# A two-layer graph network on one core: GpSimd's layer-norm step set ahead of its row sums, VectorE's aggregation set ahead by one bank

## The chip, the cores and the metric

One NeuronCore of a Trainium2 chip runs the whole kernel. The metric is the device time of one execution in microseconds (us).

## The reference, cut to what matters

The inputs are x (128 graphs, 128 nodes, 64 features), adj (128 graphs, 128x128) and small weights. Layer 0 is an edge network, layer 1 a plain aggregation; each has a layer norm ahead of it and a residual.

```
h    = relu(layernorm(x))
mask = adj > 0
# layer 0, for every graph b, node j, neighbour k, hidden channel c (192)
P = h @ (W1a + W1b) + b1 ;  Q = h @ W1b
hm[b,j] = sum over k with mask[b,j,k] of relu(P[b,j] - Q[b,k])
x1  = x + hm @ W2 + deg * b2          # deg = number of neighbours
# layer 1
h2  = relu(layernorm(x1))             # the second layer norm
out = x1 + (adj @ h2) @ W3^T
```

About 12% of the entries of adj are set, so the kernel does not compute all 128x128 edges. It ranks the neighbours of each node and gathers them by rank.

## The kernel before, in words

**Ranks and slots.** A prologue of some 55 us turns adj into codes: the rank of each neighbour within its node. Every node has 16 regular slots, worked off in four chunks (i = 0 to 3) of four slots. A chunk fills one of three PSUM ring places of two banks, two slots to a bank. Nodes with more than 16 neighbours get overflow rows of three slots (the fifth chunk, i = 4).

**One step is one graph.** Each engine runs its own `step(b, u)`, written out for b = -3 to 131, in order, and the engines meet at semaphores only. The chunks of a graph pass through three engines:

- ScalarE writes P into the four slots of a ring place (`seed`, L530), the first chunk's at i = 0 and so on. The seed of chunk 1 (L540) waits until VectorE has consumed the whole chunk 3 of the graph before.
- TensorE adds -Q of the selected neighbours, by a product with one-hot matrices in two f16 parts (`gather`, L378), eight matmuls for a chunk.
- VectorE consumes a bank (`consume`, L763): relu and sum into acc. It does bank 0, then makes a piece of the one-hot matrices of the next four graphs (`prepare`, L749), then does bank 1. At fixed places between them stand its small tasks: L790 (bn_aggr of the second layer norm's statistics), L795 and L798 (which rows belong to which overflow row, for the next graph), L804, L680, the residual additions L813 and L816, and the statistics L819.

**TensorE's order** in a step b: chunk 0, four small matmuls (L420 to L423), chunk 1, the projections of graph b+1 and output products (L435 to L445), chunks 2 and 3, then at i = 3 a block of transposes (L454 to L470), then the overflow rows (L406, then L378 with onehot_row). The block of transposes sums the acc of graph b-1 (L464) with its overflow rows (L465), and forms adj @ h2 of graph b-3 (L470). Its waits stand ahead of what needs them: all the matmuls L464 and L465 stand behind `hm_row_ready`, and L470 behind `h2_ready`.

```
pe.wait_ge(summed, b * REGULAR)
pe.wait_ge(hm_row_ready, b)
...
pe.wait_ge(h2_ready, b - 2)
```

**GpSimd's order** in a step b: the three slots of graph b-1's overflow rows are added (L864, two additions, behind ScalarE's relu L562); then the second layer norm of graph b-3 (L873 variance plus eps, L874 minus the mean, L880 the power -0.5, L883 the shift), behind `mv_ready` from L790; then the start of the next graph's acc (L851), the low part of P (L890), bias and residual (L897, L900), and the split of a later graph's h (L906, L908).

**ScalarE's order** in a step: seeds 0, copies L550 and L556, seed 1, L562, L567, L570, seeds 2 and 3, L575, L576, then L583 (h2 = relu(x1 * rstd + shift), behind `norm2_ready` from L883) and L591, and then the next graph's seed 0.

Of the kernel before, what the change touches and what calls it, by code (L numbers as in the profile page):

```python
# [30 lines left out]
ALU = mybir.AluOpType  # L31
# [7 lines left out]
ROW_SLOTS = 3  # L39
# [14 lines left out]
def gnn_kernel(nc, x, adjT, W1a, W1b, b1, W2, b2, W3T, CONSTS, out):  # L54
# [15 lines left out]
    with ExitStack() as ctx:  # L70
# [550 lines left out]
        def _(dve):  # L621
# [138 lines left out]
            def consume(u, to, bank_, first):  # L760

                sums = acc[:, u % 2]
                return nc.vector.scalar_tensor_tensor(sums, slots[to][:, bank_], 0.0, start[:, :, :] if first else sums, ALU.max,  # L763
                                                      ALU.subtract if first else ALU.add)

            def step(b, u, looped=False, t=None):
                main = exists(b)
                at = bass.ds(b + 1, 1)
                for i in range(CHUNKS):
                    if i == 3 and main and exists(b + 1):  # L770
                        dve.wait_ge(p_ready, b + 2)
                        second_part(b + 1, u + 1)
                    if main and i < REGULAR:
                        if i == 0:
                            dve.wait_ge(start_ready, b + 1)
                            if exists(b - 2):
                                dve.wait_ge(transposed, b + 2)
                        else:
                            dve.wait_ge(summed, b * REGULAR + i)
                        dve.wait_ge(gathered, b * GATHERS + i * BANKS + 1)  # L780
                        consume(u, place(u, i), 0, i == 0).then_inc(half_summed, 1)
                    if i < REGULAR:
                        prepare(b, u, i)
                    if main and i < REGULAR:
                        dve.wait_ge(half_summed, b * REGULAR + i + 1)
                        dve.wait_ge(gathered, b * GATHERS + i * BANKS + 2)
                        consume(u, place(u, i), 1, False).then_inc(summed, 1)
                    if i == 0 and exists(b - 3):
                        wait_apart(dve, stats2_ready, b - 2)
                        nc.vector.bn_aggr(mv[:, (u + 1) % 2, :], stats2[:, :]).then_inc(mv_ready, 1)  # L790
                    if i == 0 and exists(b + 1):

                        if main:
                            dve.wait_ge(owner_ready, b + 1)
                        nc.vector.tensor_scalar(from_first[:, :], count_h[:, :], first_row[:, at], None, ALU.is_ge).then_inc(from_ready, 1)  # L795
                    if i == 1 and exists(b + 1):
                        dve.wait_ge(from_ready, b + 2)
                        nc.vector.scalar_tensor_tensor(owner[:, (u + 1) % 2, :], count_h[:, :], end_row[:, at], from_first[:, :], ALU.is_lt,  # L798
                                                       ALU.mult).then_inc(owner_ready, 1)
                    if i == 2 and main:  # L800

                        dve.wait_ge(rows_ready, b + 1)
                        for s in range(ROW_SLOTS):
                            last = nc.vector.tensor_scalar(onehot_row[:, s, :], code_row[:, :], 2.0 * (COVERED + s) + 1.0, None,  # L804
                                                           ALU.is_equal)
                        last.then_inc(onehot_row_ready, 1)
                    if i == 3 and exists(b - 2):

                        dve.wait_ge(xb_ready, b - 1)
                        dve.wait_ge(mixed, b + 2)  # L810
                        if exists(b + 1):
                            dve.wait_ge(p_ready, b + 2)
                        nc.vector.tensor_tensor(x_all[:, b - 2, :], x_all[:, b - 2, :], out1_ps, ALU.add).then_inc(x1_ready, 1)  # L813
                    if i == 4 and exists(b - 4):
                        dve.wait_ge(mixed, b + 2)
                        nc.vector.tensor_tensor(x_all[:, b - 4, :], x_all[:, b - 4, :], out2_ps, ALU.add).then_inc(y_ready, 1)  # L816
                    if i == 4 and exists(b - 2):
                        wait_apart(dve, x1_ready, b - 1)
                        nc.vector.bn_stats(stats2[:, :], x_all[:, b - 2, :]).then_inc(stats2_ready, 1)  # L819
                if main and looped:  # L820
                    first, n = load(nc.vector, 0, b), load(nc.vector, 1, b)
                    with nc.vector.If(n > 0):
                        with nc.vector.Fori(0, n) as k:
                            edges = bass.ds(k * SLOTS + COVERED, SLOTS)
                            wait_apart(dve, summed, b * REGULAR + REGULAR)
                            dve.wait_ge(gathered, b * GATHERS + GATHERS)
                            nc.vector.tensor_scalar(loop_codes[:, :], count_h[:, edges], 2.0, 1.0, ALU.mult,
                                                    ALU.add).then_inc(loop_codes_ready, 1)
                            wait_apart(dve, loop_codes_ready, first + k + 1)
                            for s in range(SLOTS):  # L830
                                last = nc.vector.tensor_scalar(onehot_row[:, s, :], code_kj[:, b, :],
                                                               loop_codes[:, s:s + 1], None, ALU.is_equal)
                            last.then_inc(onehot_loop_ready, 1)
                            dve.wait_ge(loop_summed, first + k + 1)
                            dve.wait_ge(loop_gathered, first + k + 1)
                            consume(u, place(u, CHUNKS), 0, False).then_inc(loop_half_summed, 1)
                            wait_apart(dve, loop_half_summed, first + k + 1)
                            consume(u, place(u, CHUNKS), 1, False).then_inc(loop_summed, 1)
# [8 lines left out]
        def _(pool):  # L847
# [8 lines left out]
                    nc.gpsimd.tensor_scalar(start[:, 0, :], start[:, 0, :], 0.0, None, ALU.max).then_inc(start_ready, 1)  # L856

            def step(b, u, looped=False, t=None):
                if exists(b - 1):

                    pool.wait_ge(relu_row_ready, b)
                    sums = relu_row[:, 0, :]
                    for s in range(1, ROW_SLOTS):
                        last = nc.gpsimd.tensor_tensor(sums, sums, relu_row[:, s, :], ALU.add)  # L864
                        if s < ROW_SLOTS - 1:
                            last.then_inc(half_row_ready, 1)
                            pool.wait_ge(half_row_ready, (b - 1) * (ROW_SLOTS - 2) + s)
                    last.then_inc(hm_row_ready, 1)
                if exists(b - 3):

                    k = (u + 1) % 2
                    wait_apart(pool, mv_ready, b - 2)
                    nc.gpsimd.tensor_scalar(ve2[:, :], mv[:, k, 1:2], EPS, None, ALU.add).then_inc(ve2_ready, 1)  # L873
                    nc.gpsimd.tensor_scalar(neg2[:, k:k + 1], mv[:, k, 0:1], -1.0, None, ALU.mult).then_inc(neg2_ready, 1)  # L874
                    pool.wait_ge(ve2_ready, b - 2)
                    if exists(b - 4):
                        pool.wait_ge(norm2_ready, b - 3)
                    if exists(b - 5):
                        pool.wait_ge(h2_ready, b - 4)
                    nc.gpsimd.tensor_tensor(rstd2[:, k:k + 1], ve2[:, :], half_power[:, :], ALU.pow).then_inc(rstd2_ready, 1)  # L880
                    pool.wait_ge(neg2_ready, b - 2)
                    pool.wait_ge(rstd2_ready, b - 2)
                    nc.gpsimd.tensor_tensor(shift2[:, k:k + 1], neg2[:, k:k + 1], rstd2[:, k:k + 1], ALU.mult).then_inc(norm2_ready, 1)  # L883
                if exists(b + 1):

                    pool.wait_ge(p_ready, b + 2)
                    if exists(b):
                        pool.wait_ge(summed, b * REGULAR + 1)
                        start_sums(b + 1, u + 1)
                    nc.gpsimd.tensor_tensor(PQ[:, (u + 1) % 2, 1, 0:H], P[:, (u + 1) % 2, :], PQ[:, (u + 1) % 2, 0, 0:H],  # L890
                                            ALU.subtract).then_inc(p_part_ready, 1)
# [64 lines left out]
```

## Time and profile before

| what | value |
|---|---|
| median of 3 runs | 905.02 us (904.84 to 905.02) |
| the profiled execution's own time | 904.65 us |
| its span, first to last instruction | 902.6 us |
| TensorE busy | 862.0 us (96%) |
| VectorE busy | 866.4 us (96%) |
| ScalarE busy | 775.9 us (86%) |
| GpSimd busy | 698.8 us (77%) |
| granted TensorE clock, mean | 0.983 |

The span is counted from the first to the last instruction of the program; 2.05 us of the profiled execution's time lie around it. The rest of a profile is read here by step: 128 graphs pass between about 59 and 882 us, and a step is the stretch from VectorE's first consumption of one graph (the only L763 that reads `start`) to that of the next.

### The profile page before, as it was taken

The numbers are of one execution on the slowest core, as the hardware profiler recorded it, in microseconds if no ns is written. First come the engines' busy times: TensorE is split into PE (matmuls) and PEld (weight loads), VectorE is DVE, ScalarE is ACT, GpSimd is POOL, SyncE is SP. The second block draws the span as 40 slices with busy tenths as digits, with TensorE's granted clock in tenths as the row PEclk, the third lists the DMA queues.
The fourth block names the chain that finished last, engine by engine and source line by source line (L and its number), as shares of the span: only waits on it lengthen the run. The fifth ranks groups of instructions, "written<-read, shape, count | busy, mean of one in ns | idle before, by whom it ended". The sixth has DMA issues, their size and how long they took to land.

```text
span 902.6 us, 27715 instructions
## 1 busy us (share of the span) xinstructions
PE 862.0 (96%) x8626; PEld 771.7 (86%) x8627; DVE 866.4 (96%) x3032; ACT 775.9 (86%) x1728; POOL 698.8 (77%) x1548
## 2 busy tenths in 40 slices
PE   3879999999999999999999999999999999999996
PEld 1448999989998989999999999998999899989995
DVE  6989999999999999999999999999999999999993
ACT  4858989898989898989889898988898889898983
POOL 0857787888888888888887878787878788888874
PEclk9789999999999999999999999999999999999997
DMA  9700000000000000000000000000000000000000
GB/s 341 279 1 5 20 11 20 16 20 17 19 17 20 11 20 17 20 17 20 15 14 16 20 17 19 17 18 18 12 20 16 20 16 20 16 20 11 7 8 16
DMA packets 26549, 27.58 MB, mean 31 GB/s; under 512 B 3360, under 2 KB 24352, under 8 KB 25376
## 3 DMA queue, kind: packets, MB, share of 16 engines
q1 hardware_dynamic: 25488, 25.37, 8.3%
q8 instruction: 72, 1.18, 0.6%
q14 instruction: 77, 0.63, 0.2%
q10 hardware_dynamic: 912, 0.39, 0.2%
HBM read 21.56 MB, written 4.19 MB: 29 GB/s over the span
## 4 chain that ended last, share of the span: by engine, by line
PE 69%; DVE 19%; issue 5%; ACT 3%; POOL 2%; DMA 1%; SPq 0%; ACTq 0%; POOLq 0%; DVEq 0%
PE ring L378 36%; DVE acc L763 12%; PE ring L406 6%; PE post L465 4%; PE post L464 4%; PE prep L435 4%; PE post L470 4%; PE prep L445 3%; PE prep L442 2%; DVE onehot_space L749 2%; PE prep L441 2%; ACT ring L530 1%; POOL rstd L915 1%; DMA x_all<-x_nbf_dram 1%; DVE onehot_row L804 1%
## 5 line engine op out<-in xcount | busy, mean ns | idle before, releaser
L763 DVE SCALAR_TENSOR_TENSOR acc<-ring,acc 128x384 f32<-128x384 f32 x896 | 489.0, 546 | 1.1 <-PE ring L378 0.2
L530 ACT COPY ring<-P 128x768 f32<-128x768 f32 x512 | 403.3, 811 | 16.3 <-DVE acc L763 6.9
L378 PE MATMUL ring<-PQ,onehot_space 128*128 128x192 f16 x4096 | 404.0, 247 | 7.2 <-ACT ring L530 3.3
L378 PEld LDWEIGHTS ring<-PQ,onehot_space 128*128 128x128 f16 x4096 | 338.2, 100 | 31.7 <-ACT ring L530 19.2
L864 POOL TENSOR_TENSOR relu_row<-relu_row 128x192 f32<-128x192 f32 x256 | 151.8, 593 | 101.1 <-ACT relu_row L562 91.1
L749 DVE TENSOR_SCALAR onehot_space<-mask_all 128x512 f16<-128x512 f16 x512 | 155.2, 305 | 0.0
L583 ACT ACTIVATE h<-x_all,shift,rstd 128x64 f32<-128x64 f32 x128 | 56.3, 440 | 83.6 <-POOL shift L883 83.6
L851 POOL TENSOR_SCALAR start<-P,spare 128x192 f32<-128x192 f32 x128 | 121.1, 946 | 5.9 <-ACT P L576 5.1
L464 PE MATMUL post<-consts,acc 128*128 128x128 f32 x512 | 98.5, 274 | 1.5 <-POOL relu_row L864 1.5
L465 PE MATMUL post<-ownerT,relu_row 128*128 128x128 f32 x512 | 99.0, 275 | 0.0
L406 PE MATMUL ring<-PQ,owner 128*128 128x384 f16 (+1 forms) x512 | 94.1, 306 | 0.0
L880 POOL TENSOR_TENSOR rstd<-ve,half_power 128x1 f32<-128x1 f32 x128 | 89.4, 698 | 0.0
L378 PE MATMUL ring<-PQ,onehot_row 128*128 128x192 f16 x768 | 84.3, 246 | 0.4 <-DVE onehot_row L804 0.4
L562 ACT ACTIVATE relu_row<-ring 128x576 f32<-128x576 f32 x128 | 82.5, 644 | 0.6 <-PE ring L378 0.6
L763 DVE SCALAR_TENSOR_TENSOR acc<-ring,start 128x384 f32<-128x384 f32 x128 | 71.3, 557 | 11.4 <-PE ring L378 1.6
L465 PEld LDWEIGHTS post<-ownerT,relu_row 128*128 128x128 f32 x512 | 77.3, 191 | 0.0
L378 PEld LDWEIGHTS ring<-PQ,onehot_row 128*128 128x128 f16 x768 | 65.2, 98 | 9.2 <-DVE onehot_row L804 1.1
L890 POOL TENSOR_TENSOR PQ<-P,PQ 128x192 f16<-128x192 f32 x128 | 70.5, 551 | 2.7 <-ACT P L576 2.7
L406 PEld LDWEIGHTS ring<-PQ,owner 128*128 128x128 f16 x512 | 50.5, 99 | 18.2 <-issue 0.2
L575 ACT CAST PQ<-prep 128x384 f16<-128x384 f32 x128 | 63.9, 499 | 0.7 <-PE prep L437 0.7
L470 PE MATMUL post<-adj_again,h 128*128 128x128 f32 x256 | 62.0, 324 | 2.1 <-ACT h L583 2.1
L435 PE MATMUL prep<-w_parts,h1T 128*128 128x384 f16 x256 | 62.9, 328 | 0.9 <-ACT h1T L550 0.9
(129 smaller groups left out, 1616.0 us busy)
## 6 DMA issues: line engine op xcount, KB each, us to landing
onehot_space<-adj_kbj_dram SPq DMA_DIRECT2D x8, 1024.0 KB, 17.1
adj_again<-adj_kbj_dram SPq DMA_DIRECT2D x128, 64.0 KB, 1.9
x_all<-x_nbf_dram SPq DMA_DIRECT2D x8, 512.0 KB, 17.8
out_dram<-x_all SPq DMA_DIRECT2D x32, 128.0 KB, 1.7
consts<-consts_dram SPq DMA_DIRECT2D x1, 192.0 KB, 2.6
scratch<-w1a_dram ACTq DMA_DIRECT2D x2, 48.0 KB, 4.3
scratch<-w1b_dram ACTq DMA_DIRECT2D x2, 48.0 KB, 6.7
scratch<-b_dram ACTq DMA_DIRECT2D x1, 96.0 KB, 10.0
```

What stands on the lines that cost most here:

```text
L378: last = nc.tensor.matmul(to, hot(s), parts[:, part, H:2 * H], start=False, stop=(part == 1), skip_group_check=True)
L406: nc.tensor.matmul(slots[place(u, i)][:, bank_, 0:n, :], owner[:, u % 2, :], parts[:, part, 0:H].unsqueeze(1).broadcast_to([N, n, H]), sta ...
L435: nc.tensor.matmul(pq_ps, h1T[:, :], w_parts[:, part, 0:2 * H], start=(part == 0), stop=False, skip_group_check=True)
L464: nc.tensor.matmul(sums_T_ps[:, k, :], hm, ident, start=(s == 0), stop=False, is_transpose=True)
L465: last = nc.tensor.matmul(sums_T_ps[:, k, :], hm_row[:, k * N:(k + 1) * N], ownerT[:, (u + 1) % 2, :], start=False, stop=True)
L470: last = nc.tensor.matmul(sums_T_ps[:, 2, :], h2[:, :, :], adj_again[:, at, :], start=True, stop=True)
L530: return nc.scalar.copy(slots[to], src.unsqueeze(1).unsqueeze(1).broadcast_to([N, BANKS, PER_BANK, H]))
L749: return nc.vector.tensor_scalar(onehot[:, hot_of(u), i, s, :, :], code_kj[:, bass.ds(b, QUAD), :], 2.0 * (SLOTS * i + s) + 1.0, None, ALU ...
L763: return nc.vector.scalar_tensor_tensor(sums, slots[to][:, bank_], 0.0, start[:, :, :] if first else sums, ALU.max, ALU.subtract if first ...
L851: nc.gpsimd.tensor_scalar(start[:, 0, :], P[:, u % 2, :], spare[:, b:b + 1], 0.0, ALU.mult, ALU.max).then_inc(start_ready, 1)
L864: last = nc.gpsimd.tensor_tensor(sums, sums, relu_row[:, s, :], ALU.add)
L880: nc.gpsimd.tensor_tensor(rstd2[:, k:k + 1], ve2[:, :], half_power[:, :], ALU.pow).then_inc(rstd2_ready, 1)
```

## The change

GpSimd's step begins with the second layer norm of graph b-3, and the additions of the overflow rows come after it. VectorE's bn_aggr (L790) moves from behind the consumption of bank 1 of chunk 0 to behind that of bank 0. No instruction is added or removed.

```diff
@@ VectorE, step
                         dve.wait_ge(gathered, b * GATHERS + i * BANKS + 1)
                         consume(u, place(u, i), 0, i == 0).then_inc(half_summed, 1)
+                    if i == 0 and exists(b - 3):
+                        wait_apart(dve, stats2_ready, b - 2)
+                        nc.vector.bn_aggr(mv[:, (u + 1) % 2, :], stats2[:, :]).then_inc(mv_ready, 1)
                     if i < REGULAR:
                         prepare(b, u, i)
                     if main and i < REGULAR:
                         dve.wait_ge(half_summed, b * REGULAR + i + 1)
                         dve.wait_ge(gathered, b * GATHERS + i * BANKS + 2)
                         consume(u, place(u, i), 1, False).then_inc(summed, 1)
-                    if i == 0 and exists(b - 3):
-                        wait_apart(dve, stats2_ready, b - 2)
-                        nc.vector.bn_aggr(mv[:, (u + 1) % 2, :], stats2[:, :]).then_inc(mv_ready, 1)
@@ GpSimd, step
             def step(b, u, looped=False, t=None):
-                if exists(b - 1):
-
-                    pool.wait_ge(relu_row_ready, b)
-                    sums = relu_row[:, 0, :]
-                    for s in range(1, ROW_SLOTS):
-                        last = nc.gpsimd.tensor_tensor(sums, sums, relu_row[:, s, :], ALU.add)
-                        if s < ROW_SLOTS - 1:
-                            last.then_inc(half_row_ready, 1)
-                            pool.wait_ge(half_row_ready, (b - 1) * (ROW_SLOTS - 2) + s)
-                    last.then_inc(hm_row_ready, 1)
                 if exists(b - 3):
...
                     nc.gpsimd.tensor_tensor(shift2[:, k:k + 1], neg2[:, k:k + 1], rstd2[:, k:k + 1], ALU.mult).then_inc(norm2_ready, 1)
+                if exists(b - 1):
+
+                    pool.wait_ge(relu_row_ready, b)
+                    sums = relu_row[:, 0, :]
+                    for s in range(1, ROW_SLOTS):
+                        last = nc.gpsimd.tensor_tensor(sums, sums, relu_row[:, s, :], ALU.add)
+                        if s < ROW_SLOTS - 1:
+                            last.then_inc(half_row_ready, 1)
+                            pool.wait_ge(half_row_ready, (b - 1) * (ROW_SLOTS - 2) + s)
+                    last.then_inc(hm_row_ready, 1)
                 if exists(b + 1):
```

## Rows read from the trace of the kernel before

**Rows 1.** Line L763 alone: count, shortest/median/longest ns, first and last start in us.
```profile
L763 DVE SCALAR_TENSOR_TENSOR acc<-ring,start x128: 532/558/560, 58.9 to 881.7; 128x384 f32<-128x384 f32 x128
```

**Rows 2.** The waits: who waited for whom, us in total, times, longest.
```profile
ACT h L583 <- POOL shift L883: 83.6, 128, 2.8
```

**Rows 3.** Timeline of one step: start us, duration us, engine, line; idle before and releaser.
```profile
596.23 0.80 ACT L530 COPY ring<-P 128x768 f32<-128x768 f32 x1
...
596.67 0.56 DVE L763 SCALAR_TENSOR_TENSOR acc<-ring,start 128x384 f32<-128x384 f32 x1
...
597.08 0.61 PEld L378 LDWEIGHTS ring<-PQ,onehot_space 128*128 128x128 f16 x8 [0.17 <-ACT ring L530]
...
597.14 0.28 DVE L749 TENSOR_SCALAR onehot_space<-mask_all 128x512 f16<-128x512 f16 x1
...
597.68 1.27 POOL L864 TENSOR_TENSOR relu_row<-relu_row 128x192 f32<-128x192 f32 x2 [0.67 <-ACT relu_row L562]
...
597.81 0.17 DVE L790 BATCH_NORM_AGGREGATE mv<-stats 128x2 f32<-128x6 f32 x1
...
597.90 0.43 DVE L795 TENSOR_SCALAR from_first<-count_h,first_row 128x128 f16<-128x128 f16 x1
...
598.25 0.54 DVE L763 SCALAR_TENSOR_TENSOR acc<-ring,acc 128x384 f32<-128x384 f32 x1
...
598.72 0.38 DVE L749 TENSOR_SCALAR onehot_space<-mask_all 128x512 f16<-128x512 f16 x1
...
599.03 0.22 POOL L873 TENSOR_SCALAR ve<-mv 128x1 f32<-128x1 f32 x1
...
599.49 0.34 DVE L798 SCALAR_TENSOR_TENSOR owner<-count_h,end_row,from_first 128x128 f16<-128x128 f16 x1
599.53 0.73 POOL L880 TENSOR_TENSOR rstd<-ve,half_power 128x1 f32<-128x1 f32 x1
...
600.18 0.39 PE L464 MATMUL post<-consts,acc 128*128 128x128 f32 x2
...
600.40 0.19 POOL L883 TENSOR_TENSOR shift<-neg,rstd 128x1 f32<-128x1 f32 x1
...
600.63 0.44 ACT L583 ACTIVATE h<-x_all,shift,rstd 128x64 f32<-128x64 f32 x1 [0.63 <-POOL shift L883]
...
600.85 0.39 PE L465 MATMUL post<-ownerT,relu_row 128*128 128x128 f32 x2
...
601.44 0.73 PE L406 MATMUL ring<-PQ,owner 128*128 128x384 f16 x4
...
602.12 0.54 DVE L763 SCALAR_TENSOR_TENSOR acc<-ring,acc 128x384 f32<-128x384 f32 x1
...
602.70 0.80 ACT L530 COPY ring<-P 128x768 f32<-128x768 f32 x1
...
602.85 0.21 DVE L819 BATCH_NORM_STATS2 stats<-x_all 128x6 f32<-128x64 f32 x1
...
603.14 0.56 DVE L763 SCALAR_TENSOR_TENSOR acc<-ring,start 128x384 f32<-128x384 f32 x1
```

**Rows 4.** Three GpSimd lines alone, columns as in rows 1.
```profile
L864 POOL TENSOR_TENSOR relu_row<-relu_row x256: 587/593/599, 66.4 to 888.9; 128x192 f32<-128x192 f32 x128
...
L880 POOL TENSOR_TENSOR rstd<-ve,half_power x128: 569/729/738, 81.4 to 895.5; 128x1 f32<-128x1 f32 x128
...
L883 POOL TENSOR_TENSOR shift<-neg,rstd x128: 191/192/333, 82.3 to 896.2; 128x1 f32<-128x1 f32 x128
```

**Rows 5.** Timeline of the tail, where GpSimd waits for the aggregation.
```profile
894.77 0.18 DVE L790 BATCH_NORM_AGGREGATE mv<-stats 128x2 f32<-128x6 f32 x1
...
895.04 0.23 POOL L873 TENSOR_SCALAR ve<-mv 128x1 f32<-128x1 f32 x1 [1.98 <-DVE mv L790]
```

**Rows 6.** Timeline of the prologue, a long power on GpSimd beside VectorE.
```profile
51.48 5.44 POOL L915 TENSOR_TENSOR rstd<-mom,half_power 128x32 f32<-128x32 f32 x1
...
53.77 2.72 DVE L749 TENSOR_SCALAR onehot_space<-mask_all 128x512 f16<-128x512 f16 x13
```

## The prediction

> **What bounds the kernel now.** First the line of VectorE's first consumption by itself: 128 starts, 58.9 to 881.7 us, so 822.8 / 127 = 6.48 us a step [rows 1]. That is 91% of the time, and the question is what sets 6.48. Both TensorE and VectorE are 96% busy, so shares of busy time decide nothing. The waits show where ScalarE stands still: L583 waits for GpSimd's L883 in all 128 steps, 83.6 us in total [rows 2]. Whether that costs anything must be read from one step in time, from 596.67 to 603.14 (6.47 us) [rows 3]. I count from its start as 0.00.
>
> Two stalls of TensorE stand in it. The load of chunk 1 waits for ScalarE's seed (0.17 idle at 0.41). And the block of transposes: two L464 and L465 pairs start at 3.51 and 4.18 with one pair of matmuls each 0.22 (0.67 over three); the L470 pair would then start at 4.40 and L406 at 4.63, but L406 starts at 4.77. The 0.14 is L470, which had to wait for L583 (ends at 4.40, 0.04 behind GpSimd's shift) [rows 3].
>
> Which loop closes on 6.47? TensorE's chunk 1 to VectorE's next first consumption: 603.14 - 597.08 = 6.06. That consumption to the end of bank 1 of chunk 3: 602.66 - 596.67 = 5.99. From there to the load of chunk 1, through the seed: 0.04 + 0.80 + 0.05 = 0.89 (602.70 behind 602.66; 597.08 behind 597.03) [rows 3]. Together 12.94 us for two steps, 6.47 each. So this is the binding loop (call it the seed loop); the 0.14 of L470 lies in its 6.06 part and counts half. L464 itself waits for nothing today.
>
> **The change, part by part.** Nothing is added; two things move.
>
> *VectorE: L790 one bank earlier.* In the step it starts at 1.14, behind bank 1. It will start where the L749 of chunk 0 starts now, 0.47, and end at 0.64. What follows on VectorE in chunk 0 shifts by its pitch (L790 to L795, 0.09) and L795 stands again where it was, at 1.23 [rows 3]. The second bank's completion comes 0.09 later; seed 3 and L851 wait for it and run long afterwards. Cost 0.
>
> *GpSimd: the norm first.* L873 starts 0.09 behind L790's end [rows 5], at 0.73 instead of 2.36. L908, last of the step before, is over by then. L873 to L880 is 0.50, so L880 starts at 1.23. It lasts 0.57 to 0.73 [rows 4]: the long form stands in rows 3, where VectorE's L798 began 0.04 ahead of it. Now its neighbour is L795, a short instruction that starts no earlier than L880; I take 0.57, to 1.80. L883 follows 0.14 later, at 1.94, and takes 0.19 to 0.33 [rows 4]; I take 0.20, near the median: 2.14. ScalarE then has the shift at 2.2 and not at 3.92. L583's wait of 0.63 goes, h2 is there long before L470, and TensorE's 0.14 goes.
>
> *GpSimd: the additions last.* They could start at 1.01 and will start at 2.14. The pair takes 1.27 [rows 3], which gives 3.41. L798, a VectorE instruction with two inputs in SBUF, now falls among them; it may hold the second addition up by 0 to 0.16 (what it does to L880, 0.73 against 0.57 [rows 4]). I take 0.05, nearer to nothing because L798 is itself held until the first addition ends and overlaps the second only with its last part: 3.46. The Trainium skill (SBUF — State Buffer, "Who interferes with whom") says that a VectorE instruction with two SBUF inputs contends with a GpSimd one that reads SBUF; the longer form of L880 agrees.
>
> *What is late next.* L464 stands behind these additions. Its place without a wait is 3.51, or about 3.4 once the seed stall shrinks. A wait that ends just then costs more than its length: behind L583's end (601.07) the L470 pair counts as started at 601.22 (L406's 601.44 less one pair), so 0.15 [rows 3]. L464 counts as started at 3.46 + 0.15 = 3.61. From L464 to the next first consumption it is 603.14 - 600.18 = 2.96 today, less the 0.14 that L470 loses: 2.82. This closes a new loop of one step (the row loop): 3.61 + 2.82 = **6.43 us**. Behind L464 nothing but TensorE's own queue is held: overflow rows and the next chunk 0, which is inside the 2.82.
>
> *What VectorE gains.* L795 ends at 598.33, just behind the first addition (597.68 + 0.59 [rows 3, 4]), and takes 0.43; the L749 of chunk 1 ends just behind the second and takes 0.38, where that of chunk 0 takes 0.28. L795 covers a quarter of L749's elements, so alone it takes at most 0.28. With the additions gone from there, VectorE gains 0.15 + 0.10 or more, and gives back up to 0.13 at L798. The seed loop becomes (5.92 + 5.87 + 0.89) / 2 = 6.34, below the row loop: this gain stays hidden under the new wait.
>
> **The sum.** 6.47 - 6.43 = 0.04 a step; 125 steps (graphs 3 to 127) have both parts: 5.0 us. The tail, where additions and norm swap while TensorE waits, gives and takes under 1 us; I put 0. 904.65 - 5.0 = 899.7 for the profiled execution; the median lies 0.37 above it, so 900.0.
>
> Ends of the unknowns: L883 at 0.19 and no hold-up at L798 give 6.37 (892). L798's hold-up at 0.16 gives 6.54 (914) by itself.
>
> **The rivals.** (1) *No change.* The row loop stands within 0.015 of today's 6.47: the new wait takes back what L583's wait gave. It needs 0.04 more on GpSimd's chain, for instance L883 at 0.24. For it: that chain is one loop without slack. Time 905 (903.2 to 906.8).
>
> (2) *Slower: L880 in its long form.* If L795 gets ahead of L880 at 1.23, where both are due within 0.01, L880 takes 0.73 and the row loop is 6.59: + 0.12 x 125 = 15, so 920. It decides from about 0.06 more on the chain on. Against it: L795 is short, and could hold the power up less than L798 does.
>
> (3) *Much slower: the power locks VectorE out.* Then L795, beginning just behind L880, ends at 1.85 and not at 1.66; the L749 of chunk 1 begins at 2.24, meets the first addition (2.11 to 2.70) and ends at 2.85, 0.42 later than now; L798 meets the second, 0.46. VectorE's own loop, without its wait ahead of the first consumption (0.29 from L819 on, 0.13 without wait), is 6.31 and becomes 6.77: + 37, 942. Against it: 13 L749 ran in 2.72 us, 0.21 each, while a power of 5.44 us was under way [rows 6]; so a power does not hold them up, whereas an addition does (above). The Trainium skill (same page and section) states the rule without exception, that the pair is held for the whole instruction; rows 6 disagree for the power.
>
> (4) *More than forecast.* The additions are done in time (the release costs 0.05 and not 0.15, L798 nothing), and the seed loop binds at 6.34: 0.13 x 125 = 16, 889.
>
> That the change does not do what it says I rule out: the order on GpSimd is the order of its instructions.
>
> **How the numbers follow.** Forecast 0.60, rival (1) 0.17, (2) 0.13, (3) 0.03, (4) 0.07. About 0.2% (1.8 us) is what a measurement can tell from no change. Faster 0.60 + 0.07 = 0.67, same 0.17, slower 0.16. The range runs from rival (4), 889, to 911, which takes in most of L798's upper end and leaves (2) and (3) out.
>
> **What would show it.** L583 no longer waits for L883. A new entry, TensorE's L464 waiting for L864, in most steps. L790 starts 0.47 behind the first consumption, L873 0.73, L864 about 2.14. L795 falls from 0.43 to at most 0.28, and L749 of chunk 1 to 0.28. VectorE and ScalarE show new idle time; L470 and L406 follow without a gap. It is wrong if L464 shows no wait (the step should then be 6.34), if L880 is mostly 0.73, or if L795 grows beyond 0.5.

## The result and the profile after

The changed kernel takes 893.25 us (median of 4 runs, 892.48 to 893.85) against 905.02 us; the ratio is 0.987 (95% interval 0.986 to 0.988), 11.8 us less. The forecast was faster, 900.0 in a range of 889 to 911: the direction and the new bound were right, the gain more than twice what was forecast. The profiled execution took 893.06 us, its span is 890.6.

First the busy time from the page of the changed kernel, and its longest waits (who waited for whom, us in total, times, longest):

```profile
PE 852.7 (96%) x8626; PEld 764.0 (86%) x8627; DVE 840.9 (94%) x3032; ACT 783.1 (88%) x1728; POOL 682.6 (77%) x1548
```
```profile
POOL ve L863 <- DVE mv L784: 103.7, 127, 2.4
ACT ring L530 <- DVE acc L763: 69.5, 250, 1.2
DVE acc L763 <- PE ring L378: 23.2, 125, 0.5
```

L583's wait for GpSimd, 83.6 us in [rows 2], is down to 2.2 us, 3 times. GpSimd now waits for VectorE's aggregation, and VectorE's first consumption of each graph waits for TensorE (23.2 us, 125 times): VectorE has slack, TensorE is late. (In the changed file the bn_aggr is L784, the norm L863, L864, L870 and L873, and the additions L879.)

The step, as in [rows 1], from the line of the first consumption by itself (count, ns, first and last start):

```profile
L763 DVE SCALAR_TENSOR_TENSOR acc<-ring,start x128: 530/558/559, 58.9 to 869.3; 128x384 f32<-128x384 f32 x128
```

(869.3 - 58.9) / 127 = 6.381 us, against 6.479. The difference of 0.098, 127 times, is 12.4 us; the span became 12.0 shorter. So the gain is all in the steps. Nearly all of them are alike: most steps of the changed kernel are 6.36 or 6.37 us long.

One step in time, 505.20 to 511.58 (6.38 us), the counterpart of [rows 3]:

```profile
505.20 0.56 DVE L763 SCALAR_TENSOR_TENSOR acc<-ring,start 128x384 f32<-128x384 f32 x1 [0.17 <-PE ring L378]
...
505.68 0.17 DVE L784 BATCH_NORM_AGGREGATE mv<-stats 128x2 f32<-128x6 f32 x1
...
505.94 0.22 POOL L863 TENSOR_SCALAR ve<-mv 128x1 f32<-128x1 f32 x1 [0.78 <-DVE mv L784]
...
506.41 0.26 DVE L795 TENSOR_SCALAR from_first<-count_h,first_row 128x128 f16<-128x128 f16 x1
506.43 0.57 POOL L870 TENSOR_TENSOR rstd<-ve,half_power 128x1 f32<-128x1 f32 x1
...
507.05 0.28 DVE L749 TENSOR_SCALAR onehot_space<-mask_all 128x512 f16<-128x512 f16 x1
...
507.15 0.23 POOL L873 TENSOR_TENSOR shift<-neg,rstd 128x1 f32<-128x1 f32 x1
...
507.33 1.27 POOL L879 TENSOR_TENSOR relu_row<-relu_row 128x192 f32<-128x192 f32 x2
507.72 0.35 DVE L798 SCALAR_TENSOR_TENSOR owner<-count_h,end_row,from_first 128x128 f16<-128x128 f16 x1
...
508.30 0.48 ACT L583 ACTIVATE h<-x_all,shift,rstd 128x64 f32<-128x64 f32 x1
...
508.57 0.22 PE L454 MATMUL post<-ident_h,h_parts 128*128 128x128 f16 x1
...
508.75 0.41 PE L464 MATMUL post<-consts,acc 128*128 128x128 f32 x2
...
509.00 0.39 PE L465 MATMUL post<-ownerT,relu_row 128*128 128x128 f32 x2
...
509.66 0.39 PE L470 MATMUL post<-adj_again,h 128*128 128x128 f32 x2
...
509.88 0.73 PE L406 MATMUL ring<-PQ,owner 128*128 128x384 f16 x4
...
511.58 0.56 DVE L763 SCALAR_TENSOR_TENSOR acc<-ring,start 128x384 f32<-128x384 f32 x1 [0.17 <-PE ring L378]
```

From the first consumption at 0: L784 at 0.48, L863 at 0.74, L870 at 1.23, L873 at 1.95, the additions from 2.13 to 3.40. L795 fell from 0.43 to 0.26 and the L749 of chunk 1 from 0.38 to 0.28. L406 follows L470 by 0.22, the pitch of a pair: that stall is gone. L464 starts 0.15 behind the end of the additions (508.60), and the pair behind it (L465) follows after 0.25 instead of 0.22, so it counts as started at 3.58. From there to the next first consumption it is 2.80. 3.40 + 0.18 + 2.80 = 6.38: the row loop of the prediction closes on the measured step.

The second of the two additions by itself:

```profile
508.00 0.60 POOL L879 TENSOR_TENSOR relu_row<-relu_row 128x192 f32<-128x192 f32 x1
```

L798 ends at 508.07, so it runs beside this addition for its first 0.07 us; the addition takes 0.60 all the same, and the longest of all 256 additions of the changed kernel is 0.602 us.

### The profile page after: what moved, and what is told of

Its sections match the earlier page's. It is cut to its first block, busy times and chain, and to the rows that moved or that the text cites. A ratio compares the mean times of both kernels' runs of the same rounds, so it can differ in the third digit from the quotient of the medians.

```text
span 890.6 us, 27715 instructions
## 1 busy us (share of the span) xinstructions
PE 852.7 (96%) x8626; PEld 764.0 (86%) x8627; DVE 840.9 (94%) x3032; ACT 783.1 (88%) x1728; POOL 682.6 (77%) x1548
## 4 chain that ended last, share of the span: by engine, by line
POOL 72%; issue 19%; PE 2%; DVE 2%; POOLq 1%; DMA 1%; ACT 1%; SPq 0%; ACTq 0%; DVEq 0%
POOL relu_row L879 15%; POOL start L851 14%; POOL rstd L870 8%; POOL PQ L890 7%; POOL h_parts L906 5%; POOL x_all L900 5%; POOL h_parts L908 4%; POOL bias L897 4%; POOL neg L864 3%; POOL shift L873 3%; POOL ve L863 3%; DMA x_all<-x_nbf_dram 1%; PE ring L357 1%; DVE acc L763 1%; PE ring L348 1%
## 5 line engine op out<-in xcount | busy, mean ns | idle before, releaser
L763 DVE SCALAR_TENSOR_TENSOR acc<-ring,acc 128x384 f32<-128x384 f32 x896 | 488.7, 545 | 1.0 <-PE ring L378 0.2
L378 PEld LDWEIGHTS ring<-PQ,onehot_space 128*128 128x128 f16 x4096 | 337.8, 100 | 19.3 <-ACT ring L530 3.2
L879 POOL TENSOR_TENSOR relu_row<-relu_row 128x192 f32<-128x192 f32 x256 | 151.7, 593 | 13.2 <-ACT relu_row L562 3.1
L749 DVE TENSOR_SCALAR onehot_space<-mask_all 128x512 f16<-128x512 f16 x512 | 150.8, 297 | 0.0
L851 POOL TENSOR_SCALAR start<-P,spare 128x192 f32<-128x192 f32 x128 | 131.4, 1027 | 5.7 <-ACT P L576 5.5
L863 POOL TENSOR_SCALAR ve<-mv 128x1 f32<-128x1 f32 x128 | 28.7, 224 | 103.8 <-DVE mv L784 103.7
L464 PE MATMUL post<-consts,acc 128*128 128x128 f32 x512 | 101.3, 279 | 2.7 <-POOL relu_row L879 2.4
L465 PE MATMUL post<-ownerT,relu_row 128*128 128x128 f32 x512 | 99.0, 275 | 0.0
L763 DVE SCALAR_TENSOR_TENSOR acc<-ring,start 128x384 f32<-128x384 f32 x128 | 71.3, 557 | 24.4 <-PE ring L378 23.0
L406 PE MATMUL ring<-PQ,owner 128*128 128x384 f16 (+1 forms) x512 | 93.9, 306 | 0.0
L562 ACT ACTIVATE relu_row<-ring 128x576 f32<-128x576 f32 x128 | 82.5, 644 | 0.6 <-PE ring L378 0.6
L465 PEld LDWEIGHTS post<-ownerT,relu_row 128*128 128x128 f32 x512 | 77.3, 191 | 0.0
L870 POOL TENSOR_TENSOR rstd<-ve,half_power 128x1 f32<-128x1 f32 x128 | 73.5, 574 | 0.0
L464 PEld LDWEIGHTS post<-consts,acc 128*128 128x128 f32 x512 | 58.2, 142 | 16.4 <-issue 4.1
L890 POOL TENSOR_TENSOR PQ<-P,PQ 128x192 f16<-128x192 f32 x128 | 70.2, 548 | 2.7 <-ACT P L576 2.7
L556 ACT COPY sums_T<-post 128x384 f32<-128x384 f32 (+2 forms) x130 | 62.5, 481 | 6.8 <-PE post L470 6.8
L804 DVE TENSOR_SCALAR onehot_row<-code_row 128x128 f16<-128x128 f16 x384 | 67.8, 229 | 0.0
L406 PEld LDWEIGHTS ring<-PQ,owner 128*128 128x128 f16 x512 | 50.3, 98 | 18.0
```

Of the source, the lines that this page charges most:

```text
L378: last = nc.tensor.matmul(to, hot(s), parts[:, part, H:2 * H], start=False, stop=(part == 1), skip_group_check=True)
L406: nc.tensor.matmul(slots[place(u, i)][:, bank_, 0:n, :], owner[:, u % 2, :], parts[:, part, 0:H].unsqueeze(1).broadcast_to([N, n, H]), sta ...
L464: nc.tensor.matmul(sums_T_ps[:, k, :], hm, ident, start=(s == 0), stop=False, is_transpose=True)
L465: last = nc.tensor.matmul(sums_T_ps[:, k, :], hm_row[:, k * N:(k + 1) * N], ownerT[:, (u + 1) % 2, :], start=False, stop=True)
L562: nc.scalar.activation(relu_row[:, :, :], row_slots[place(u, -1)], ACT.Relu).then_inc(relu_row_ready, 1)
L749: return nc.vector.tensor_scalar(onehot[:, hot_of(u), i, s, :, :], code_kj[:, bass.ds(b, QUAD), :], 2.0 * (SLOTS * i + s) + 1.0, None, ALU ...
```

## The experiments

Two theories at first. **A**: the changed kernel is bound by the row loop, as forecast. **B**: it got faster because VectorE was freed, and the wait at L464 is only a by-product. Ratios are to the kernel before on the same chip; that kernel ran at 905 us on some chips and at up to 907.6 on others, so the ratio is the thing to read. A step is (last start - first start) / 127 of the first consumption. Where an edit adds or takes lines, a line's number in its profile is shifted by one or more; the text gives both where it matters. "(before)" marks an edit of the kernel before; all others are edits of the changed kernel, but for "vector alone", which is the kernel before with one of the two moves.

| run | ratio, 95% interval | us | step |
|---|---|---|---|
| vector alone | 0.9995 (0.9985 to 1.0005) | 907.6 | 6.488 |
| GpSimd alone | 1.080 (1.079 to 1.082) | 980.2 | 7.067 |
| wait at the rows | 0.976 (0.974 to 0.977) | 885.3 | 6.325 |
| h2 unheld (before) | 0.995 (0.994 to 0.997) | 903.8 | 6.488 |
| powers for additions (before) | 0.992 (0.991 to 0.994) | 900.5 | 6.442 |
| L795 earlier (before) | 1.000 (0.999 to 1.001) | 907.6 | 6.497 |
| second addition a power (before) | 1.016 (1.014 to 1.018) | 922.0 | 6.615 |
| powers and h2 unheld (before) | 0.992 (0.991 to 0.994) | 899.2 | 6.450 |
| aggregation first | 1.086 (1.085 to 1.088) | 985.6 | 7.103 |
| changed kernel again | 0.985 (0.984 to 0.987) | 892.0 | 6.376 |
| no negation | 0.979 (0.977 to 0.981) | 886.6 | 6.325 |
| no negation, wait at the rows | 0.976 (0.975 to 0.978) | 883.6 | 6.315 |

### The two halves of the change

VectorE's half alone:

```diff
                         consume(u, place(u, i), 0, i == 0).then_inc(half_summed, 1)
+                    if i == 0 and exists(b - 3):
+                        (bn_aggr)
                     if i < REGULAR:
                         prepare(b, u, i)
...
-                    if i == 0 and exists(b - 3):
-                        (bn_aggr)
```

> The kernel before with VectorE's part of the change alone: L790 behind bank 0, GpSimd's order as before. Theory A (in the changed kernel a loop of one step binds: aggregation, norm, additions, L464, next first consumption) and theory B (the changed kernel got faster because VectorE was freed of the additions, and the wait at L464 is only a by-product) both expect no change, 905 us, since GpSimd still adds first: L873 behind the additions as before, L795 at 0.43. A third reading, that the earlier aggregation brings the gain by itself, expects 893.

Nothing changed, as both theories said: in GpSimd's order the wait for the aggregation stands behind the additions.

GpSimd's half alone is the changed kernel with the bn_aggr put back behind bank 1.

> The changed kernel with L790 back behind bank 1. The norm on GpSimd then starts 0.67 us later in the step. Theory A: the loop has no slack, so all of it is paid in every step: 6.37 + 0.67 = 7.04 us a step, 893 + 0.67 x 125 = 977 us. Theory B: TensorE's delay lies in the two-step loop over ScalarE's seed and counts half: 6.70 a step, 935 us.

The kernel became 8% slower. Timeline of one step of it:

```profile
504.99 0.17 DVE L790 BATCH_NORM_AGGREGATE mv<-stats 128x2 f32<-128x6 f32 x1
...
505.25 0.22 POOL L863 TENSOR_SCALAR ve<-mv 128x1 f32<-128x1 f32 x1 [1.39 <-DVE mv L790]
...
506.69 1.25 POOL L879 TENSOR_TENSOR relu_row<-relu_row 128x192 f32<-128x192 f32 x2
...
508.09 0.41 PE L464 MATMUL post<-consts,acc 128*128 128x128 f32 x2 [0.74 <-POOL relu_row L879]
```

The step is 7.067, 0.69 more than in the changed kernel, for a norm that starts 0.66 later (1.40 behind the first consumption, at 503.85 here, against 0.74). Theory A had 7.04, theory B 6.70. The step grew by all of that, so the chain has no slack, and TensorE's wait stands open at L464. So each half alone is worth nothing or 8% the wrong way; only together do they gain.

### The wait moved behind the transposes

```diff
                             pe.wait_ge(summed, b * REGULAR)
-                            pe.wait_ge(hm_row_ready, b)
...
                                     nc.tensor.matmul(sums_T_ps[:, k, :], hm, ident, ...)
+                                if k == 0:
+                                    pe.wait_ge(hm_row_ready, b)
                                 last = nc.tensor.matmul(sums_T_ps[:, k, :], hm_row[...], ownerT[...], ...)
```

> The changed kernel with TensorE's wait for hm_row_ready moved from ahead of the first L464 to ahead of the first L465, the first matmul that reads the sums; 0.22 us of matmuls that need no sums then lie ahead of the wait. Theory A: the loop gets 0.22 of slack, and the next loop binds, the two-step one over the seed: (5.91 + 5.80 + 0.89) / 2 = 6.30 us a step, 885 us; L464 follows L454 without a gap. Theory B: no change, 893 us, 6.37 a step.

885.3 us, ratio 0.976, against a forecast of 885 (0.978). The step is 6.325, for 6.30. Timeline (L463 is L464 here):

```profile
504.96 0.22 PE L454 MATMUL post<-ident_h,h_parts 128*128 128x128 f16 x1
505.02 0.39 PE L463 MATMUL post<-consts,acc 128*128 128x128 f32 x2
505.24 0.39 PE L466 MATMUL post<-ownerT,relu_row 128*128 128x128 f32 x2
```

L463 follows L454 by 0.06 instead of 0.18. Nothing on VectorE or GpSimd was touched, so theory B fell: the wait at L464 was the bound of the changed kernel.

### What bound the kernel before

The kernel before, with L583 freed of the norm:

```diff
-                        wait_apart(act, norm2_ready, b - 2)
+                        wait_apart(act, x1_ready, b - 2)
...
-                        nc.scalar.activation(..., bias=shift2[:, k:k + 1], scale=rstd2[:, k:k + 1])
+                        nc.scalar.activation(..., bias=shift1[:, bass.ds(b - 3, 1)], scale=rstd1[:, bass.ds(b - 3, 1)])
```

> The kernel before, whose L583 no longer waits for the second norm: it reads the scale and shift of the first layer norm (so the output has the second norm's statistics wrong), and waits for x1 alone. GpSimd computes the second norm as before, so the additions still collide with VectorE. This prices L583's lateness alone. The reading of the kernel before (two-step loop over the seed, 0.14 of L470 counts half): 6.40 us a step, 896 us. If that 0.14 lay in a one-step loop: 6.33, 887 us. If VectorE alone bound the kernel: 905 us.

The time fell by 0.5%, but the step is 6.488, just that of the run with VectorE's half alone, which is as fast as the kernel before. The gain lies behind the last graph: 18.2 us from the last first consumption to the end of the span (902.0 - 883.8) against 22.1 in that run (905.6 - 883.5). In the steps L583's lateness was worth **nothing**, not the 0.07 of the prediction. The timeline says where the freed time went:

```profile
502.41 1.26 POOL L864 TENSOR_TENSOR relu_row<-relu_row 128x192 f32<-128x192 f32 x2 [0.67 <-ACT relu_row L562]
502.45 0.60 DVE L795 TENSOR_SCALAR from_first<-count_h,first_row 128x128 f16<-128x128 f16 x1
...
502.98 0.54 DVE L763 SCALAR_TENSOR_TENSOR acc<-ring,acc 128x384 f32<-128x384 f32 x1
503.44 0.39 DVE L749 TENSOR_SCALAR onehot_space<-mask_all 128x512 f16<-128x512 f16 x1
```

VectorE comes earlier to L795, and the first addition holds it the longer, 0.60 for 0.43. This is **theory C**: a loop of one step over the collision, in which GpSimd's additions hold VectorE up. In [rows 3] it can be closed: seed 1 starts at 596.23 and takes 0.80; the additions start 0.65 behind it (L562 lies between) and end at 598.95; the L749 of chunk 1 ends 0.15 behind them; VectorE works from there to the end of chunk 3 in 3.56 (602.66); the next seed 1 follows by 0.04. 0.80 + 0.65 + 1.27 + 0.15 + 3.56 + 0.04 = 6.47, with no slack anywhere.

It is not the only loop that closes there. Between L583 and the next seed 1 (602.70 in [rows 3]) ScalarE of the kernel before stands still nowhere:

```profile
600.97 0.42 ACT L591 ACTIVATE h<-x_all,shift,rstd 128x64 f32<-128x64 f32 x1
601.30 0.79 ACT L530 COPY ring<-P 128x768 f32<-128x768 f32 x1
...
602.03 0.25 ACT L550 CAST h1T<-post 128x128 f16<-128x128 f32 x1
...
602.19 0.47 ACT L556 COPY sums_T<-post 128x384 f32<-128x384 f32 x1
```

Seed 1 at 596.23, through L562, the additions and the norm to L583 at 600.63, is 4.40; from there to the next seed 1 it is 2.07; together 6.47 again. Call it the loop through L583. The run with h2 unheld opened this one and the steps stayed as they were, so it was not the only bound of that length.

Test of C: L795 moved ahead of the L749 of chunk 0, where GpSimd is idle.

```diff
                         consume(u, place(u, i), 0, i == 0).then_inc(half_summed, 1)
+                    if i == 0 and exists(b + 1):
+                        (L795, from_first)
                     if i < REGULAR:
                         prepare(b, u, i)
```

> The kernel before with L795 moved ahead of the L749 of chunk 0, where GpSimd is idle, so that the first addition cannot hold it up (0.22 for 0.43). The prediction's reading (two-step seed loop) takes half of the 0.21 off each step: 6.37, 892 us. Theory C: the L749 of chunk 1 is then earlier, waits for the end of the second addition as before, and all behind it stays where it was: no change, 905 us, with that L749 at 0.6 and not 0.38.

No change, as C said and the prediction's reading did not. The loop through L583 does not contain L795 either and says the same, so this run speaks against the seed loop but does not tell those two apart. Timeline (L786 is L795 here, and its L795 is the bn_aggr):

```profile
502.21 0.25 DVE L786 TENSOR_SCALAR from_first<-count_h,first_row 128x128 f16<-128x128 f16 x1
...
502.81 1.26 POOL L864 TENSOR_TENSOR relu_row<-relu_row 128x192 f32<-128x192 f32 x2 [0.68 <-ACT relu_row L562]
...
503.63 0.59 DVE L749 TENSOR_SCALAR onehot_space<-mask_all 128x512 f16<-128x512 f16 x1
504.14 0.55 DVE L763 SCALAR_TENSOR_TENSOR acc<-ring,acc 128x384 f32<-128x384 f32 x1
```

The L749 takes 0.59 and ends at 504.22, 0.15 behind the additions (504.07). What L795 saved, that L749 lost.

Then the hold itself: both additions replaced by powers on one element, in the same place.

```diff
-                        last = nc.gpsimd.tensor_tensor(sums, sums, relu_row[:, s, :], ALU.add)
+                        last = nc.gpsimd.tensor_tensor(junk[:, s - 1:s], ones[:, 0:1], half_power[:, :], ALU.pow)
```

> The kernel before with each of GpSimd's two additions of overflow slots replaced by a power on one element per partition into a tile of its own (the output lacks the overflow rows' second and third slots). It takes about as long (0.57 for 0.59 us) and stands at the same place, but rows 6 say that it does not hold VectorE up. Theory C, formed from the run with h2 unheld: in the kernel before a loop of one step binds, which runs over the collision: VectorE's chunk 3, seed 1, L562, both additions, the L749 of chunk 1 that they hold up, and VectorE to chunk 3 again. It expects L795 at 0.22 to 0.25, the L749 of chunk 1 at 0.28, L583's wait still there, and some 6.33 us a step where the seed loop binds: 887 us. If GpSimd's time bound the kernel and not its hold on VectorE: 905 us.

```profile
501.76 0.55 POOL L891 TENSOR_TENSOR PQ<-P,PQ 128x192 f16<-128x192 f32 x1
502.07 0.40 DVE L750 TENSOR_SCALAR onehot_space<-mask_all 128x512 f16<-128x512 f16 x1
...
504.42 1.20 POOL L865 TENSOR_TENSOR junk<-ones,half_power 128x1 f32<-128x1 f32 x2 [0.67 <-ACT relu_row L563]
...
504.64 0.22 DVE L796 TENSOR_SCALAR from_first<-count_h,first_row 128x128 f16<-128x128 f16 x1
...
505.24 0.28 DVE L750 TENSOR_SCALAR onehot_space<-mask_all 128x512 f16<-128x512 f16 x1
```

The powers hold nothing: L796 (L795) takes 0.22, the L750 (L749) of chunk 1 0.28. But the step fell to 6.442 only, a third of the 0.14 or so expected. The first two rows show why: the last L750 of the step now runs into L891 (L890) and takes 0.40, ending 0.16 behind it. GpSimd's chain, which starts at L562, caught VectorE further down.

The second addition alone replaced by a power, the first kept:

> The kernel before with the second addition alone replaced by a power (the output lacks the overflow rows' third slot). Theory C: L795 stays at 0.43, the L749 of chunk 1 falls from 0.38 to 0.28, and the loop closes over the first addition, 0.10 shorter: 6.37, 893 us. The seed loop would give half of it: 6.42, 899 us.

This missed by the most: 1.6% slower, where 1.3% faster was expected. Timeline (L866 is the first addition, L868 the power, L878 the negation):

```profile
503.28 0.59 POOL L866 TENSOR_TENSOR relu_row<-relu_row 128x192 f32<-128x192 f32 x1 [0.67 <-ACT relu_row L563]
...
503.95 0.68 POOL L868 TENSOR_TENSOR junk<-ones,half_power 128x1 f32<-128x1 f32 x1
504.31 0.28 DVE L750 TENSOR_SCALAR onehot_space<-mask_all 128x512 f16<-128x512 f16 x1
...
505.03 0.38 POOL L878 TENSOR_SCALAR neg<-mv 128x1 f32<-128x1 f32 x1
...
506.33 0.95 POOL L852 TENSOR_SCALAR start<-P,spare 128x192 f32<-128x192 f32 x1
```

Held the other way round, GpSimd's small instructions are stretched where VectorE's run beside them: 0.68 for 0.57, 0.38 for 0.23. The chain became 0.16 longer (from the first addition at 503.28 to L852, which is L851, at 506.33 it is 3.05, against 2.89 in the kernel before, 597.68 to 600.57) and the step 0.13 longer than in the run with VectorE's half alone. So GpSimd's whole chain was in the loop, and not the additions alone. By which way it closed, through L583 or through VectorE behind L851 and L890, this run does not say.

Powers for both additions and h2 unheld, together:

> The kernel before with powers for both additions and with h2 unheld (the edits of two earlier runs together; the output lacks the overflow rows' second and third slots and the second norm's statistics). The run with powers stopped at 6.44 us a step. Two loops over GpSimd's chain are left there: through L583's wait, and through VectorE's last L749 of the step, which L890 holds up (0.395 for 0.28), and L804 behind L851. If L583's wait binds there: 6.31, 0.975 of before. If the hold-up by L851 and L890 binds there, at the end of the same chain that starts at L562: no change in the step, 6.44, and only the 4 us of the tail that the run with h2 unheld gained, 0.988 of before.

```profile
503.73 0.55 POOL L891 TENSOR_TENSOR PQ<-P,PQ 128x192 f16<-128x192 f32 x1
...
504.03 0.40 DVE L750 TENSOR_SCALAR onehot_space<-mask_all 128x512 f16<-128x512 f16 x1
...
504.92 0.80 ACT L531 COPY ring<-P 128x768 f32<-128x768 f32 x1 [0.49 <-DVE acc L764]
```

The step stays at 6.450. The ratio, 0.992, is not the 0.988 of the second case either: the tail is 3.1 us shorter than in the run with powers (19.3 against 22.4), but the steps take 1.0 us of that back. ScalarE now waits for VectorE ahead of seed 1, and VectorE is still held by L891 (L890). So L583's wait did not hold the run with powers by itself; of the two loops named, the one through L851 and L890 is left. For the kernel before it fits this picture: GpSimd's chain begins at L562, ends at L890, and VectorE runs into it at one place or another; take one collision away and the next one binds. What is shown is that neither the seed loop nor the loop through L583 was the bound by itself. That theory C was the one beside them rests on the closed sum and on the ends that follow each other; no run opened it without another loop at nearly the same length.

### Beyond the change

The aggregation one bank earlier still, ahead of the first consumption:

> The changed kernel with L790 one bank earlier still, ahead of the first consumption. By the row loop alone the additions end 0.6 us earlier, TensorE's wait at L464 goes, and the step is 6.31 (885 us) as with the wait moved. Theory C with the collision says otherwise: the additions then run from about 1.5 to 2.8, hold up the L749 of chunk 1 (due at 1.75) to about 2.27, and L790 stands behind its own input L819 with 0.13 lost; VectorE's own loop is then some 6.46, 905 us.

Theory C had the sign against the changed kernel and not the size: it had 905 us, and the run is 8.6% slower than the kernel before, with a step of 7.10.

```profile
502.23 1.26 POOL L879 TENSOR_TENSOR relu_row<-relu_row 128x192 f32<-128x192 f32 x2
502.29 0.68 DVE L749 TENSOR_SCALAR onehot_space<-mask_all 128x512 f16<-128x512 f16 x1
...
504.80 0.55 POOL L890 TENSOR_TENSOR PQ<-P,PQ 128x192 f16<-128x192 f32 x1
504.83 0.91 DVE L804 TENSOR_SCALAR onehot_row<-code_row 128x128 f16<-128x128 f16 x3
```

The first addition holds the L749 of chunk 1 by 0.4 (0.68 for 0.28, to 0.15 behind that addition's end at 502.82), and L890 and L897 hold L804 by 0.5 (0.91 for 0.38 without a hold). Only the first had been reckoned with. Of the three places tried for the aggregation on the changed kernel, the one behind bank 0 is the best.

The changed kernel once more, and a shorter norm (the negation dropped):

```diff
-                    nc.gpsimd.tensor_scalar(neg2[:, k:k + 1], mv[:, k, 0:1], -1.0, None, ALU.mult).then_inc(neg2_ready, 1)
...
-                    nc.gpsimd.tensor_tensor(shift2[:, k:k + 1], neg2[:, k:k + 1], rstd2[:, k:k + 1], ALU.mult).then_inc(norm2_ready, 1)
+                    nc.gpsimd.tensor_scalar(shift2[:, k:k + 1], mv[:, k, 0:1], rstd2[:, k:k + 1], -1.0, ALU.mult, ALU.mult).then_inc(norm2_ready, 1)
```

> The changed kernel again, on the chip of the two runs beside it. Ratio to the kernel before as in the result, 0.987 (0.984 to 0.989), 6.37 us a step.

> The changed kernel with GpSimd's norm one instruction shorter: the negation goes and the shift is made from mean, scale and -1 in one tensor_scalar. A dose against the loop of one step: its chain is 0.19 shorter (the pitch of the negation), less what the new form costs more (0 to 0.1). Theory A: TensorE's wait at L464 (0.14 in the changed kernel) goes, the two-step seed loop binds, 6.31 as in the run with the wait moved: 0.978 of before. If another loop held 6.37: 0.987. Theory C adds a doubt: L851 starts 0.19 earlier and can now hold up the L749 of chunk 2, which would give back up to 0.1 a step.

> The wait for the sums at L465 and the shorter norm together. Theory A: the loop of one step is then off the bound by 0.4, and nothing is gained over the wait moved alone, 0.976 of before, 6.31 a step, unless the shorter chain moves a collision: L804 and the last L749 of the step are held up by 0.14 and 0.09 in that run, behind L851 and L890, which now end 0.1 to 0.2 earlier. If these go, the seed loop is shorter by half of 0.2: 6.21, 0.962. If L749 of chunk 2 is hit instead: 6.35, 0.982.

0.985 again for the changed kernel. Without the negation 0.979 and 6.325 a step: the same bound that moving the wait reached, from the other side of the row loop. Both together, 0.976 and 6.315, add nothing clear of the intervals to the wait moved alone. So the next loop lies at 6.31 to 6.33; the seed loop of the prediction gives 6.30 there. That it is this loop was worked out and not tried by itself. One thing in the run with the wait moved fits a loop of two steps: its steps alternate, most of them 6.22 to 6.24 and then 6.36 to 6.44, where those of the changed kernel are all alike. The version with the wait at L465 beats both kernels, 0.976 of before.

## Why the prediction was right or wrong

**Right: the new bound.** L464 behind the additions became the bound and capped the gain; the run with the wait moved and that with GpSimd's half alone show it with sizes of 885.3 for 885 and 0.69 a step for 0.67. The times of the chain, from the first consumption, were right as well, the forecast in brackets: L863 at 0.74 (0.73), L870 at 1.23 (1.23) and 0.57 long (0.57), L873 at 1.95 (1.94), the additions from 2.13 (2.14).

**Wrong: the size, by the hold-up put on the second addition.** "I take 0.05 ... 3.46" was the term. The second addition was not held up at all: they end at 3.40. L798 takes 0.35 against 0.34 and ends 0.15 behind the first addition (508.07, 507.92), only 0.07 into the second one, which takes its usual 0.60. The prediction had seen that overlap rightly and priced it too high, after the 0.16 that L798 does to L880. In [rows 3] L798 lies 0.30 beside L880 (599.53 to 599.83); whether it is the shorter overlap or the other instruction that spares the addition, no run shows. The other terms nearly cancel: the release of L464 cost 0.18, not 0.15, and the stretch behind it 2.80, not 2.82. Together 6.38 and not 6.43. The step before, put at the 6.47 of one step, was 6.479 in the mean, which gives the last 0.01. The forecast gain was the small difference of two large numbers, 6.47 and 6.43, and 0.05 of error in it is more than the whole: measured 0.098 a step, forecast 0.04. The prediction's own lower end, 6.37 and 892 with no hold-up, is close to where the kernel came out, 6.38 and 893.

**Wrong, without consequence for the sum: what bound the kernel before.** The prediction closed a two-step loop over the seed on 6.47 and took that as the bound, with L470's 0.14 counting half. The run with h2 unheld shows that L583's wait was worth nothing in the steps. The run with L795 earlier shows that 0.2 less on VectorE in the seed loop was worth nothing too. At least one other loop of the same length stood there; a one-step loop over the collision of GpSimd's chain with VectorE closes on it. The prediction saw L795 and L749 end just behind the additions and counted that only as a gain hidden in the kernel to come; on the account above it was a part of what held the kernel before. The sum stood because the time after is set by the row loop alone.

**Of the rivals:** no change needed 0.04 more on GpSimd's chain, which came out 0.06 shorter (3.40 for 3.46). Slower (L880 at 0.73) did not come: L870 has a median of 0.573, and L795 starts 0.02 ahead of it and does not hold it. The power does not lock VectorE out: L795 takes 0.26 beside it, and 0.22 in the run with powers, where it begins well inside one. "More than forecast" (889) would have needed the wait at L464 to vanish; the run with the wait moved takes it away and reaches 885.3. That rival had put the hold-up at L798 at nothing, which was right, and the cost of the release at 0.05, which measured 0.18.

**Wrong as a sign to look for:** "a new entry, TensorE's L464 waiting for L864, in most steps". The waits of the changed kernel have only 3 such, 2.4 us in total. A wait of 0.12 shows as the distance L454 to L464 (0.18 for 0.06) and as VectorE's new wait for TensorE, not as an entry of its own.

## What to carry to other kernels

Where two engines alternate on a shared resource, a long chain on the slower one can be the bound at any point where the other runs into it; to find out, look for instructions whose ends follow the other engine's ends by a constant, and close the loop through them. A loop that closes on the measured step is not yet the bound when a second one closes too: remove one wait alone and see. And place a wait directly ahead of what reads the data: here one line moved behind two transposes gave 1% more, and when a forecast gain is the difference of two near loops, its range must be that of the loops, not of the gain.

## What the runs showed of the hardware

GpSimd's additions on 128x192 elements (L864, L879) and its L890 hold up a VectorE instruction with f16 in and out in SBUF until just before their own end: where the L749 meets one of them, it ends 0.15 or 0.16 behind it in all the rows shown. Not every GpSimd instruction of that size does it so: in the step of the kernel before, three L804 run in 0.38 us inside the 0.95 us of L851 (600.57 to 601.52). A power on one element of each partition does not hold it, though two of them take 1.20 us against the 1.27 of two additions (0.22 for L795 beside them).

The Trainium skill (SBUF — State Buffer, "Who interferes with whom") says of VectorE's 2-port modes that whoever issues first has the shared port pair for the whole instruction and the other blocks fully; for the additions, L890 and L749 the trace nearly agrees (alone the L749 takes 0.28, and it ends 0.15 behind the one that held it), and for the powers it does not. It also says that the order of issue decides who blocks; the run with one addition replaced agrees for GpSimd's negation, which starts at 505.03, 0.05 behind VectorE's L799 (L798, 504.98), and takes 0.38 for 0.23.
